# A gated cross-attention and MoE layer on one core: all output projections behind the last group, a fifth slot of probabilities, key tiles weighted two to a run

## The reference

```python
def attention(q, k, v):                    # 16 heads of 32
    scores = jnp.einsum('bqhd,bkhd->bhqk', q, k) * scale
    probs = jax.nn.softmax(scores, axis=-1)
    return jnp.einsum('bhqk,bkhd->bqhd', probs, v)
q = rms_norm(linear(x, q_w, q_b), norm_q_w)...
# keys and values of 257 image and 1344 text rows have weights and a norm of their own
out = (attention(q, k, v) + attention(q, k_img, v_img)).reshape(B, L, DIM)
return linear(out, o_w, o_b)
...
x = x + tanh(g_xattn[0]) * xattn(layernorm(x), ctx, ...)
x = x + tanh(g_ffn[0]) * ffn(layernorm(x), ...)   # 8 experts, 2 of them a token, and a shared one
```

## Time and profile before

| engine | busy us | share of the span |
|---|---|---|
| TensorE, matmuls | 1668.2 | 98% |
| TensorE, weight loads | 1119.6 | 65% |
| VectorE | 1184.7 | 69% |
| GpSimd | 900.4 | 53% |
| ScalarE | 831.6 | 49% |

### The profile page before, as it was taken

One profiled execution on the slowest core, in us unless ns is written; L12 is line 12 of the kernel. 1 busy time (PEld: TensorE's weight loads), 2 busy tenths in 40 slices (PEclk: granted clock), 3 DMA queues, 4 the chain that ended last, 5 costly groups with the idle time before them and its releaser, 6 DMA issues. The chain is left out here.

```text
span 1710.4 us, 24784 instructions
## 1 busy us (share of the span) xinstructions
PE 1668.2 (98%) x8694; PEld 1119.6 (65%) x8694; DVE 1184.7 (69%) x2220; ACT 831.6 (49%) x1550; POOL 900.4 (53%) x343
## 2 busy tenths in 40 slices
PE   6999999999999999999999999998999999999999
PEld 5888878886445555455554455445777778888777
DVE  6776677667888887888878888777444454443565
ACT  4443333326666664666556666662221355554221
POOL 3221311215777775788747777710605476775642
PEclk9999999999999999999999999999999999999999
DMA  9556858646556553565455555211314487886533
GB/s 332 167 158 195 242 173 210 195 151 195 154 153 159 147 149 66 154 159 159 137 139 145 157 136 141 101 39 42 136 38 155 163 267 258 271 270 198 174 103 99
DMA packets 198603, 277.34 MB, mean 162 GB/s; under 512 B 30968, under 2 KB 128008, under 8 KB 197964
## 3 DMA queue, kind: packets, MB, share of 16 engines
q1 hardware_dynamic: 192928, 258.91, 51.4%
q0 software_dynamic: 5120, 16.78, 2.9%
q10 hardware_dynamic: 432, 0.07, 0.0%
HBM read 202.21 MB, written 106.42 MB: 180 GB/s over the span
## 5 line engine op out<-in xcount | busy, mean ns | idle before, releaser
L1306 ACT ACTIVATE P<-ps 128x512 f32<-128x512 f32 (+1 forms) x832 | 444.8, 598 | 232.8 <-PE ps L1147 160.3
L1437 DVE TENSOR_REDUCE mp<-ps 128x1 f32<-128x448 f32 x720 | 411.8, 615 | 80.3 <-PE ps L1127 78.2
L1587 POOL TENSOR_TENSOR sacc<-sacc,P 128x2048 f32<-128x2048 f32 x90 | 397.7, 4419 | 16.4 <-ACT P L1306 5.5
L1127 PE MATMUL ps<-Kst,Qst 96*128 96x448 f32 x960 | 336.1, 371 | 2.7 <-DVE stl L626 1.7
L1147 PE MATMUL ps<-Qst,Kst 100*128 100x512 f32 (+1 forms) x832 | 323.5, 411 | 4.0 <-ACT P L1306 3.2
L1127 PEld LDWEIGHTS ps<-Kst,Qst 96*128 96x128 f32 x960 | 182.9, 191 | 156.7 <-DVE mp L1437 86.5
L1081 PE MATMUL ps<-P,Vg 128*32 128x512 f32 (+2 forms) x1664 | 217.5, 607 | 0.4 <-ACT P L1306 0.3
L822 POOL TENSOR_TENSOR cl<-craw,ch 128x1024 fp32r<-128x1024 f32 (+2 forms) x26 | 62.0, 2383 | 283.2 <-ACT ch L550 283.2
L1147 PEld LDWEIGHTS ps<-Qst,Kst 100*128 100x128 f32 (+1 forms) x832 | 153.1, 186 | 71.4 <-ACT P L1306 40.2
L49 PE MATMUL ps<-W,ch 128*128 128x512 f32 (+1 forms) x408 | 162.5, 398 | 0.0
L51 PE MATMUL ps<-W,cl 128*128 128x512 f32 (+1 forms) x408 | 159.7, 392 | 0.0
(11 more groups left out here) (249 smaller groups left out, 3145.1 us busy)
## 6 DMA issues: line engine op xcount, KB each, us to landing
gur<-in_w_gate_up SPq DMA_DIRECT2D x23, 1024.0 KB, 7.7
Kst<-KHd SPq DMA_DIRECT2D x56, 320.0 KB, 4.9
Vd<-vf SPq DMA_DIRECT2D x50, 256.0 KB, 2.1
craw<-in_ctxT SPq DMA_DIRECT2D x24, 512.0 KB, 4.4
KHd<-sth SPq DMA_DIRECT2D x24, 512.0 KB, 3.5
KLd<-stl SPq DMA_DIRECT2D x24, 512.0 KB, 4.9
dnr<-in_w_down SPq DMA_DIRECT2D x23, 512.0 KB
xg<-Xg SPq DMA_DIRECT2D x23, 512.0 KB, 7.9
```

The lines of the kernel that those rows point to most:

```text
L1127: ins = pe.matmul(ps[:, bank, 0:c1 - c0], Qst[G % 3][0:96, j, 128 * qt:128 * qt + 128], Kst[s][0:96, j, c0:c1], start=True, stop=True)
L1306: act.activation(P[slot(G, kt)][:m, j, :], ps[:m, 2 + (e - 1) % 3, :], ACT.Exp, scale=SCALE).then_inc(a_exp, 1)
L1437: dve.reduce_max(out, ps[:, bank:bank + k, 0:cols] if k > 1 else ps[:, bank, 0:cols], AX.X).then_inc(d_ra, 1)
L1587: pool.tensor_tensor(sacc[:, h], sacc[:, h], P[slot(G, kt)][:, h], ALU.add).then_inc(g_sum, 1)
```

## The change

- The projection of all four batches is moved behind the last group: 16 tiles one after another, in PSUM banks 0 and 1 by turns; `PROJECTED`, the splits in the groups and the ring's places for projections go. The transposes of tiles 0 to 3 stand behind tiles 6 and 7.
- Each group's normalised result is stored to a new DRAM tensor `Ad` (SP, step 1, two groups later). A batch of four is loaded back whole (128 x 2048) and split by one ScalarE copy and one GpSimd subtraction. Batch 0 is loaded in step 3 of group 15 and split behind its step 6; batches 1 and 2 are loaded behind the last totals; batch 3 has batch 1's place and is loaded once tile 7 is projected.
- The last group's results are worked out at full width (512) and not in quarters, stored and loaded like the others.
- The memory of `aTh` and `aTl` goes to a fifth slot of probabilities (`slot` divides by `NP` = 5).
- Tile 1 stays with tile 0 in step 3; tiles 2 and 3 are weighted in step 5, 4 and 5 in step 7, 6 and 7 in step 9, and tile 8 in front of 9 and 10 in step 11. Steps 4, 6, 8 and 10 have no weighting.

```diff
     def slot(G, kt):
-        return (NKT * G + kt) % 4
+        return (NKT * G + kt) % NP
...
+    def store_result(G):
+        sp.wait_ge(g_oi, 3 * G + 3) if G < NG - 1 else sp.wait_ge(d_last, 5)
+        sp.dma_start(Ad[G // 4, 128 * (G % 4):128 * (G % 4) + 128, :], ot2[:, G % 2, :]).then_inc(s_at, 16)
+
+    def load_results(b):
+        sp.wait_ge(s_at, 16 * (4 * b + 4))
+        sp.dma_start(AR[b][:], Ad[b].rearrange("(k p) s -> p k s", p=128)).then_inc(s_a[b % 2], 16)
...
+            if kt == 1 and 2 <= G <= NG:
+                store_result(G - 2)
+            if step == LASTG + 3:
+                sp.wait_ge(p_sc, exp_no(NG - 2, 12, 3))
+                load_results(0)
...
+    def pe_project_tile(k):
+        b, t = divmod(k, 4)
+        if t == 0:
+            pe.wait_ge(a_ath, b + 1)
+            pe.wait_ge(g_atl, b + 1)
...
+        pe.wait_ge(d_ra, LAST_RA + max(0, k - 1))
         for kk in range(4):
-            ins = mm3(ps[:, bank, :], a_high(4 * b + kk)[:, 128 * t:128 * t + 128], a_low(4 * b + kk)[:, 128 * t:128 * t + 128],
+            ins = mm3(ps[:, k % 2, :], AH[b][:, kk, 128 * t:128 * t + 128], AL[b][:, kk, 128 * t:128 * t + 128],
...
         def text_end(G):
+            weigh(G, 8, 0, 128, False, False)
             weigh(G, 9, 0, 128, False, False)
...
-            if 3 <= kt < 11:
+            if kt == 3:
+                weigh(G, 1, 0, 128, False, False)
+            if kt in (5, 7, 9):
+                weigh(G, kt - 3, 0, 128, False, False)
                 weigh(G, kt - 2, 0, 128, False, False)
...
-            if G in PROJECTED and kt in (4, 6, 8, 10):
...
-        project_last(0)
-        project_last(1)
-        pe_across(0)
...
+        for k in range(NT):
+            pe_project_tile(k)
+            if k in (6, 7):
+                pe_across(2 * k - 12)
+                pe_across(2 * k - 11)
...
+    def results_high(b):
+        act.wait_ge(s_a[b % 2], 16 * (b // 2 + 1))
+        if b == 3:
+            act.wait_ge(p_ra, LAST_RA + 8)
+        act.activation(AH[b][:], AR[b][:], ACT.Copy).then_inc(a_ath, 1)
...
-            if j == 0 and NKT * G + kt >= 4:
-                fG, fk = divmod(NKT * G + kt - 4, NKT)
+            fG, fk = divmod(NKT * G + kt - NP, NKT)
+            if j == 0 and fG >= 0:
...
+            if step == LASTG + 6:
+                results_high(0)
...
+        results_high(1)
+        results_high(2)
+        root_of_variance_act(0)
+        for k in range(4):
+            act_across(k)
+        root_of_variance_act(1)
+        results_high(3)
...
+        dve.reciprocal(rt[:, 0, :], ps[:, TOTALS, :]).then_inc(d_last, 1)
...
+        dve.reciprocal(rt[:, 1, :], ps[:, LAST_IMAGE, :]).then_inc(d_last, 1)
...
+        for k in range(NT):
+            dve_project_tile(k)
...
+            if k in (7, 8):
+                dve_across(2 * k - 14)
+                dve_across(2 * k - 13)
...
+        def results_low(b):
+            pool.wait_ge(a_ath, b + 1)
+            pool.tensor_tensor(AL[b][:], AR[b][:], AH[b][:].bitcast(F32), ALU.subtract).then_inc(g_atl, 1)
...
+        sp.wait_ge(d_add, 4 * (NG - 1) + 9)
+        load_results(1)
+        load_results(2)
+        store_result(NG - 1)
...
+        load_gu(1)
+        load_dn(1)
+        sp.wait_ge(p_ra, LAST_RA + 8)
+        load_results(3)
```

More of the change, by code:

```diff
@@ L119, in program @@
     a_txt, a_img, g_oi, d_inv = sem("a_txt"), sem("a_img"), sem("g_oi"), sem("d_inv")
-    a_ath, d_atl = sem("a_ath"), sem("d_atl")
+    s_at, s_a, a_ath, g_atl = sem("s_at"), [sem(f"s_a{i}") for i in range(2)], sem("a_ath"), sem("g_atl")
     d_st3 = sem("d_st3")
@@ L217, in rows_ra @@
     def rows_ra(G):
-        return 64 + 65 * G + 4 * sum(x < G for x in (5, 9))
+        return 64 + 65 * G
     def head_rows(d, G, c0, c1):
@@ L244, in program @@
     oi = sb(p2, "oi", [128, D], F32)
+    Woh = sb(p2, "Woh", [128, 4, D], F32R)
+    Wol = sb(p2, "Wol", [128, 4, D], F32R)
+    P.append(sb(p2, "P4", [128, 4, LQ], F32))
     p2.close()
-    p2w = ExitStack()
-    sb(p2w, "front", [128, 4 * NKP + 2 * NKT * 128 + 32 + 4 * 4 * LQ + 88 + 3 * 4 * LQ], F32)
-    wo = sb(p2w, "wo", [128, 4, D], F32)
-    p2w.close()
+    NP = len(P)
+    p2b = ExitStack()
+    A2h = sb(p2b, "A2h", [128, 4, LQ], F32R)
+    A2l = sb(p2b, "A2l", [128, 4, LQ], F32R)
+    sb(p2b, "front", [128, 27888 - 4096 - 1104 + 4096], F32)
+    A1h = sb(p2b, "A1h", [128, 4, LQ], F32R)
+    A1l = sb(p2b, "A1l", [128, 4, LQ], F32R)
+    p2b.close()
+    p2r = ExitStack()
+    sb(p2r, "above2", [128, 2048], F32)
+    A2r = sb(p2r, "A2r", [128, 4, LQ], F32)
+    sb(p2r, "above0", [128, 16000], F32)
+    A0r = sb(p2r, "A0r", [128, 4, LQ], F32)
+    sb(p2r, "abovew", [128, 6688], F32)
+    wo = sb(p2r, "wo", [128, 4, D], F32)
+    sb(p2r, "above1", [128, 2048], F32)
+    A1r = sb(p2r, "A1r", [128, 4, LQ], F32)
+    p2r.close()
+    AR = [A0r, A1r, A2r, A1r]
+    AH, AL = [Qst[1], A1h, A2h, A1h], [Qst[2], A1l, A2l, A1l]
     p1r = ExitStack()
@@ L1301, in exps @@
                     act.wait_ge(p_tot, tot_no(fG, fk))
[L1302 to L1303 removed]
+            if j == 3 and fk == 7 and 0 <= fG < NG - 1:
+                act.wait_ge(d_add, 4 * fG + 1)
             e = exp_no(G, kt, j)
@@ L1370, in act_attend, with dve_project_tile @@
                     act.activation(hi, early, ACT.Copy).then_inc(a_early, 1)
[L1371 to L1393 removed]
+        results_high(1)
[5 more added lines that the diff above has]
+        results_high(3)
+        root_of_variance_act(2)
+        root_of_variance_act(3)
+    def dve_project_tile(k):
+        dve.wait_ge(p_ra, LAST_RA + k + 1)
+        dve.scalar_tensor_tensor(acc[:, k, :], ps[:, k % 2, :], tg[:, 0:1], acc[:, k, :], ALU.mult, ALU.add).then_inc(d_ra, 1)
+        dve.wait_ge(d_ra, LAST_RA + k + 1)
         dve.bn_stats(st3[:, k, 0:6], acc[:, k, :]).then_inc(d_st3, 1)
@@ L1484, in dve_attend @@
                     sum_of_last(kt - 1)
-                if kt == 12:
-                    split(G - 1)
-            elif kt == 2 and 2 <= G < NG:
-                units(G + 1, at, sum(plan))
-                split(G - 2)
-                if G == NG - 1:
-                    sum_of_last(1)
+            elif kt == 2 and G == NG - 1:
+                sum_of_last(1)
             elif kt == 11:
@@ L1513, in dve_attend @@
                     dve.tensor_tensor(lo, early, hi.bitcast(F32), ALU.subtract).then_inc(d_early, 1)
-            if step == NKT * NG:
-                for b in range(NB - 1):
-                    variance(b)
         G = NG - 1
-        rt, ot = rt2[:, 1, :], ot2[:, G % 2, :]
-        def results_of_last(t):
-            cs = slice(128 * t, 128 * t + 128)
-            dve.reciprocal(rt[:, cs], ps[:, LAST_IMAGE, cs]).then_inc(d_last, 1)
-            dve.wait_ge(d_last, 4 * t + 9)
-            dve.tensor_tensor(oi[:, cs], ps[:, PV, cs], rt[:, cs], ALU.mult).then_inc(d_last, 1)
-            dve.wait_ge(d_last, 4 * t + 10)
-            dve.tensor_tensor(oi[:, cs], oi[:, cs], ot[:, cs], ALU.add).then_inc(d_last, 1)
-            dve.wait_ge(a_ath, NG + t)
-            dve.tensor_tensor(a_low(NG - 1)[:, cs], oi[:, cs], a_high(NG - 1)[:, cs].bitcast(F32), ALU.subtract).then_inc(d_last, 1)
-        def project_last(t):
-            dve_project_tile(NB - 1, t, ra + t, TAIL_BANKS[t])
+        rt, ot = rt2, ot2[:, G % 2, :]
         dve.wait_ge(a_txt, 2 * G + 1)
@@ L1611, in pool_attend @@
                     pool.tensor_tensor(Wol[:, k], wo[:, k], Woh[:, k].bitcast(F32), ALU.subtract).then_inc(g_wol, 1)
+            if step == LASTG + 6:
+                results_low(0)
             if kt == 12 and 1 <= G < NG:
                 normalise(G - 1)
+        for b in range(1, NB):
+            results_low(b)
     sp_attend()
@@ L1721, in store_rows @@
             sp.dma_start(Yg[128 * j:128 * j + 128, :], yr[:, j % 2, :]).then_inc(s_y[j % 2], 16)
-        for q in range(1, 4):
+        load_gu(1)
+        load_dn(1)
+        sp.wait_ge(p_ra, LAST_RA + 8)
+        load_results(3)
+        for q in range(2, 4):
             load_gu(q)
```

142 lines of the change are left out of this document (27 added, 115 removed).

## The result

The changed kernel takes 1714.16 us (median of 22 runs, 1711.39 to 1720.73), the kernel before in the same comparison 1712.43. The ratio over the single runs is 1.0018, 95% interval 1.0009 to 1.0026; that of the two medians alone is 1.0010. One of the 22 runs of the kernel before took 4242.84 us, and the ratio leaves it out. The profiled execution took 1713.28 us, with a span of 1712.0, 1.6 more than the kernel before. The forecast of 1716.7 (1.0019 of 1713.42) was near, but the result is made of large terms of opposite sign, so I read each.

What follows compares the result with a forecast made beforehand. TensorE was taken to bound the groups, other engines counting only where they make it wait. Terms of +4.5 (groups 0 to 14), -25.1 (groups 5 and 9) and +23.9 (group 15, tail) gave +3.3: 1716.7 us, range 1698 to 1727.

Steps and rivals of the forecast that it cites:

- What bounds the groups: Groups: only TensorE's time counts, other engines only where they make it wait; busy, 45.57 of 45.70 us, hides waits.
- The price of a run, 0.32 us: Groups 0 to 14, steps 3 to 11: nine runs become five, 4 x 0.32 = 1.28 us less per group.
- The new stalls, 1.8 us: Stretches between runs, steps 4 to 11: TensorE waits for VectorE's reductions, 1.8 us per group; bounds 0.9 and 2.4.
- The fifth slot, -0.2 us: Groups: one more slot removes ScalarE's waits for slots, 0.2 us less per group; bounds 0 and 0.5.
- Net of the groups: Groups 0 to 14: 15 x (0.5 - 0.2) = +4.5 us, bounds -5 and +12.
- Groups 5 and 9: Without four projection tiles each falls from 58.1 to its neighbour's 45.6 us: -25.1 us together.
- Group 15, -7.0: Last group: ScalarE becomes the bound, 23.0 in place of 30.0 us, totals end 7.0 earlier; bounds 4 and 10.
- The tail, +30.9: End of the totals to the feed-forward part: projections, transposes, waits and clock make 52.4 in place of 21.5 us.
- The clock: Tail: half clock behind three waits of 1.1 to 2.0 us, 1.5 us allowed; 5.1 if every wait did it.
- Maxima keep up (1690): Rival, groups: VectorE stays ahead, new stalls don't come, 15 x -1.5 = -22 us, 1690; chance for this side 0.27.
- Batches late (1726): Rival, tail: loads of batches 1 and 2 share engines, the first takes up to 13.8 us, 1726; chance 0.22.
- Pairing saves nothing (1735): Rival, groups: a run's cost goes with its first tile's shape, stalls still come, +19 us, 1735; chance 0.06.

Runs made afterwards that it cites:

- after_half: The changed kernel with each of VectorE's maxima in the groups taken over half of the unit's keys: 1696.1 us, 0.9921 of the kernel before.
- tail_single: The changed kernel with the pairing undone, one tile weighted in each of steps 4 to 10: 1700.34 us, 0.9954 of the kernel before.
- pairs_only: The kernel before with the pairing alone (new places of the runs, four slots, projections and tail as before): 1715.73 us, 1.0039 of the kernel before.
- across_later: The changed kernel with tile 3's transpose in the tail one projection tile later, behind tile 8: 1711.36 us, 1.0003 of the kernel before.
- eight_across: The changed kernel with tiles 2 to 7 one to a step and tile 3's transpose one projection tile later: 1701.24 us, 0.9934 of the kernel before.
- tail_single_4: `tail_single` with four slots of probabilities in place of five: 1706.86 us, 0.9967 of the kernel before.
- eight_late: `tail_single` with tile 8 alone moved into step 11's run: 1704.01 us, 0.9943 of the kernel before.
- single_across_order: `tail_single` with tile 3's transpose one projection tile later and VectorE adding projection tiles 0 and 1 among the last results: 1702.46 us, 0.9937 of before.

## Why the prediction held, step by step

**What bounds the groups.** Right. TensorE is the bound and "busy" hides its stalls: 45.49 of 45.82 us are busy, and yet `after_half` does the same group in 44.7.

**The price of a run, 0.32 us.** Right; `after_half` against `tail_single` gives 1.28 for four. That is the sum; how it divides into 0.13, 0.11 and 0.10 is read from rows of the kernel before and no run tests it. The Trainium skill (TensorEngine Tiling (Array Packing), Key Properties) speaks of a drain at a change of mode. With the 0.09 to 0.10 of the front edge alone the four would be 0.4 us; the runs show three times that, so the measurement decides: what stands in the run itself and behind it counts too.

**The new stalls, 1.8 us.** Right: 1.85. (The four differences as I printed them add up to 1.9, 18.55 less 16.65; the measured stretches add up to 18.61.) The stretches between the runs of group 8 are 4.50, 4.94, 4.64 and 4.53 us, worked out as 4.5, 4.9, 4.6 and 4.55. The rule (a unit behind the reduction four units earlier, with VectorE at 0.53 and 0.33) came from one stretch of the kernel before. Its limit: with three banks and single runs it was 0.4 us a group short.

**The fifth slot, -0.2 us.** Right as a sum (step 12 from 6.3 to 6.1), but I had given it to the slot. The slot takes 0.12 away where the runs are single, and tile 8's move takes the 0.2 away without it (`pairs_only`). So in the changed kernel the slot adds nothing to an ordinary group that a run shows.

**Net of the groups.** An ordinary group went from 45.47 to 45.82, +0.35, where +0.3 was worked out; for 15 groups and with groups 5 and 9 -20.9 against -20.6.

**Groups 5 and 9.** -12.2 each (58.10 to 45.86), as far as the group's own growth lets it. The neighbour's 45.6 that I worked with is not in the row, which has 45.70; by the row the term is -24.8 and not -25.1.

**Group 15, -7.0.** The size is right (-7.1), and the waits fit its cause, ScalarE as the bound: TensorE's weight loads for scores wait for it 35 times in group 15, 16.0 us together. No run tests it. One piece I had only in the bounds: GpSimd's subtraction of the first batch took 6.33 us in place of 4.62, beside VectorE's additions. And 3.4 us of half clock stand in step 3, which I had not spoken of; the kernel before has them in the same step (4.98 us long, 4.97 in the changed kernel), so they are no part of the difference. `tail_single`, which has none, does step 3 in 3.34. Windows of group 15 up to the first projection, `tail_single`, the changed kernel, `across_later` (the third column from the end is the clock):

```profile
1075.75:1120.46 44.71, 41.30 (x228) 12.59 (x228) 32.92 (x14) 32.94 (x60) 17.43 (x6) 1.00 0.38 131
```

```profile
1083.74:1129.42 45.68, 43.10 (x229) 13.27 (x229) 33.02 (x14) 32.78 (x60) 17.52 (x6) 0.96 0.39 128
```

```profile
1083.96:1132.93 48.97, 46.88 (x229) 14.39 (x229) 33.02 (x14) 32.95 (x60) 17.52 (x6) 0.86 0.34 120
```

The last two do the same work, and the length follows the clock: 10.2 us more of half clock, 3.3 us longer.

**The tail, +30.9.** Measured +30.0; each term:
- The wait ahead of tile 2 was 1.02, forecast 1.5.
- The wait for batch 1, forecast 1.1, did not come. The load was sized at 6.9 by a load of the same size; these took 5.5. This is the term that was furthest off, and it was close: GpSimd ended at 1141.91 and tile 4 began at 1142.01.

```profile
A1r<-Ad SPq DMA_DIRECT2D x2, 1024.0 KB, 5.5
A2r<-Ad SPq DMA_DIRECT2D x1, 1024.0 KB, 8.0
```

- The wait ahead of the fourth transposed tile was 2.24, forecast 2.0.
- The clock: half clock from 1157.90 to 1161.3, which cost 1.7 us, where I had allowed 1.5 for all waits together.
- Batch 3 came in time: GpSimd ended at 1165.98, tile 12 began at 1169.94. The forecast had 0.1 us of room there; it came to that only once the waits ahead of it were taken away, in `eight_across`.

**The rivals.** Maxima keep up (1690): no; `after_half` is what it would look like, and even that reached only 0.9921, since GpSimd's sums come next, a limit that this rival's sum left out. Batches late (1726): no, but not for the reason given. I had called the DMA queues nearly empty there, against the earlier trace rows, which has a share of 0.70; in the changed kernel it is 0.84 from 1129.42 to 1137.50, at 286 GB/s. Of the two loads issued together only the second was held up, 8.0 us, and neither took the 13.8 of the rival. Pairing saves nothing (1735): no, by the 1.28.

**How much of it was luck.** Little in the number, more in two reasons: the fifth slot and the empty DMA queues were wrong grounds for terms that came out right. No large term was wrong: the four stretches missed by -0.3, -0.1, -0.9 and -0.2 us, all to the same side, so the errors did not hide each other. Inside the tail they did in part (-0.5 and -1.1 against +0.2 and +0.2). That the ratio lies nearer to the forecast (1.0018 against 1.0019) than the spans do (+1.6 us against +3.3) is chance. The highest of my three chances, 0.41, was on slower than can be told; the measured 0.18% lies just below the 0.2% that I drew as the line.

The Trainium skill (TensorE: Matmul & The Clock Gate, HAM oscillation) tells of a kernel whose waits of 3 to 5 us between its stretches of matmuls let the clock fall again each time. The waits here are shorter. In the tail the wait of 2.24 us was followed by half clock in all seven kernels profiled with it (the changed one, `tail_single`, `tail_single_4`, `eight_late`, `after_half` and the two with three banks), and so was that of 2.01 in `single_across_order`; the wait of 1.0 was not, in any of the ten kernels that have it. Had every wait done it, as in the 5.1 us of the prediction, the two waits that came would have cost 3.4 us in the tail; the rows give 1.7.

## What to carry to other kernels

Work between two stretches that another engine must keep up with is not only a cost: a run of other matmuls gives that engine time to catch up. Before removing such a run, count how many units then follow one another against the buffers between the engines, and step the slower engine's cadence through them unit by unit; the average over the stretch says that there is time where there is none. And a change made of a gain and a loss should be split before it is judged: here the part without pairing is 0.5% faster, and the pairing gives it back. Where it gives it back was shown by taking time off VectorE and by taking a bank away, and not by the pairing alone.
